# Taking a routing stage apart: choices inside the output stage, counts inside the first expert chunks, a residual add on GpSimd

## What is computed

```python
x = x + layernorm(attention(layernorm(x)))      # 16 heads, prefix mask
t = layernorm(x).reshape(-1, 256)
scores = softmax(t @ gate_w.T)                  # 8 experts
idx = top_k(scores + gate_b, 2)[1]              # the two best
cw = sum(one_hot(idx) * scores[idx])            # a weight per token and expert
y_e = swiglu((t @ w1_e.T + b1_e) * (t @ w3_e.T + b3_e)) @ w2_e.T + b2_e
out = x + layernorm(sum_e(cw_e * y_e) + shared_expert(t))
```

## Time and profile before

| | |
|---|---|
| time before, median of 3 runs | 2312.86 us (2309.55 to 2316.68) |
| the profiled execution, its own time | 2297.38 us |
| its span, from first to last instruction | 2295.6 us |
| TensorE matmul, busy | 2074.2 us, 90% |
| ScalarE, busy | 1701.4 us, 74% |
| VectorE, busy | 1521.9 us, 66% |
| GpSimd, busy | 645.4 us, 28% |
| output stage, about | 1253 to 1406 us |
| routing stage, about | 1406 to 1443 us |
| expert stage, matmuls | 1443 to 2234 us |

### The profile page before, as it was taken

How to read it: one execution, slowest core, us unless ns; L and a number is a source line. 1 busy time by engine, 2 the same in 40 slices (tenths; PEclk the granted TensorE clock), 3 DMA queues, 4 the chain that set the end, 5 groups by cost and what they waited for, 6 DMA issues and landing times. The chain is left out here.

```text
span 2295.6 us, 38125 instructions
## 1 busy us (share of the span) xinstructions
PE 2074.2 (90%) x14085; PEld 1267.4 (55%) x14085; DVE 1521.9 (66%) x2352; ACT 1701.4 (74%) x2162; POOL 645.4 (28%) x639
## 2 busy tenths in 40 slices
PE   5995999999999999999998794799999999999970
PEld 4783333333333333333332784688888888888860
DVE  4664255555555555555555896677789988998875
ACT  4663999999999999999997672433466666666645
POOL 1111000000000000000000451677345565555637
PEclk9997999999999999999999996899999999999995
DMA  5886655555444456555410682455567676677756
GB/s 184 307 290 194 139 104 105 105 102 90 73 87 87 90 100 105 105 102 75 58 37 21 220 272 108 164 179 173 193 194 208 179 179 176 173 182 178 175 167 254
DMA packets 162651, 340.50 MB, mean 148 GB/s; under 512 B 17768, under 2 KB 91624, under 8 KB 155176
## 3 DMA queue, kind: packets, MB, share of 16 engines
q1 hardware_dynamic: 130220, 284.42, 46.5%
q0 software_dynamic: 29936, 45.90, 10.7%
q10 hardware_dynamic: 2316, 7.80, 1.0%
HBM read 194.29 MB, written 143.62 MB: 147 GB/s over the span
## 5 line engine op out<-in xcount | busy, mean ns | idle before, releaser
L1108 ACT ACTIVATE att_prob<-att_scores 128x1024 f32<-128x1024 f32 (+2 forms) x1122 | 997.7, 1031 | 58.5 <-PE att_scores L1054 54.9
L1073 PE MATMUL att_out<-att_prob,att_va 128*32 128x512 f32 (+3 forms) x5000 | 576.5, 541 | 12.9 <-DVE att_prob L1140 12.9
L1054 PE MATMUL att_scores<-att_qs,att_ks 50*128 50x512 f32 (+3 forms) x2560 | 465.5, 430 | 21.2 <-DMA att_qs<-guard 17.1
L1054 PEld LDWEIGHTS att_scores<-att_qs,att_ks 50*128 50x128 f32 x2560 | 210.9, 185 | 492.5 <-ACT att_prob L1108 417.9
L1776 POOL DMA_INDIRECT sums<-moe_y,moe_token x142 | 290.9, 2048 | 265.5 <-ACT moe_y L2034 225.2
L1918 PE MATMUL moe_ps<-moe_xt_hi,moe_w_hi 128*128 128x512 f32 (+1 forms) x880 | 339.8, 386 | 10.1 <-ACT moe_h L2007 7.1
L1918 PE MATMUL moe_ps<-moe_xt_hi,moe_w_lo 128*128 128x512 f32 (+1 forms) x880 | 333.4, 379 | 0.0
L1918 PE MATMUL moe_ps<-moe_xt_lo,moe_w_hi 128*128 128x512 f32 (+1 forms) x880 | 331.9, 377 | 0.0
L1002 POOL DMA_DIRECT2D ctx_scr<-att_cout x64 | 55.1, 860 | 983.0 <-DVE att_cout L1190 944.1
L1140 DVE SCALAR_TENSOR_TENSOR att_prob<-att_prob,att_tri 128x512 f32<-128x512 f32 x224 | 144.8, 688 | 269.0 <-ACT att_prob L1108 269.0
L1073 PEld LDWEIGHTS att_out<-att_prob,att_va 128*32 128x32 f32 x5000 | 108.3, 108 | 186.3 <-issue 105.5
(11 more groups left out here) (259 smaller groups left out, 3257.5 us busy)
## 6 DMA issues: line engine op xcount, KB each, us to landing
qk_parts<-proj_qk SPq DMA_DIRECT2D x64, 512.0 KB, 4.2
keep_first_weights<-w_experts SPq DMA_DIRECT2D x22, 1412.0 KB, 6.6
moe_wraw<-w_experts SPq DMA_DIRECT2D x21, 1412.0 KB, 6.8
att_qs<-qk_parts SPq DMA_DIRECT2D x180, 128.0 KB
att_ks<-qk_parts SPq DMA_DIRECT2D x180, 128.0 KB
rows_in<-att_zeros SPq DMA_DIRECT2D x13, 1632.0 KB, 21.6
moe_rows<-rows_in SPq DMA_DIRECT2D x22, 544.0 KB, 3.8
proj_xin<-x SPq DMA_DIRECT2D x16, 512.0 KB, 3.8
```

Source lines behind the costliest of these rows:

```text
L1054: last = nc.tensor.matmul(pss[e % SBUFS][:, h, at:at + CH - q0], ks[s][rows, half, kt * P:(kt + 1) * P], qs[s][rows, half, c * CH + q0:(c ...
L1073: last = nc.tensor.matmul(pso[k % 2][strip, q0:], va[team % 2][:, kt, strip], probs_of(u)[:, h, at:at + CH - q0], start=(kt == 0), stop=(i ...
L1108: nc.scalar.activation(probs_of(u)[:, half * 2:half * 2 + 2, start:], pss[e % SBUFS][:, :, start:], ACT.Exp, scale=HD ** -0.5)\
```

## The change

- The routing stage is gone. Its tiles become pieces of one tile `late` (class `Routing`), which later is the place of sums.
- In the output stage VectorE makes softmax and choices for groups of 16 tiles (four chunks, 128x128 elements): for groups 0, 1 and 2 in steps 9 to 12, 13 to 16 and 17 to 20, behind `context_lo`: two instructions in the first of the four steps, then four, six and seven. The last group gets only its first two there. The logits lie in two PSUM tiles by turns. ScalarE takes the exponential of each group.
- The residual add goes from VectorE to GpSimd, as the last thing of GpSimd's step: `residual(k - NORM)`, that is chunk k-2. VectorE begins its step with `measure_sum(k-3)`, which waits for that.
- The first weights are loaded in step 2, the first rows in step 6, and the first weights are cut into parts in steps 17 and 18 (`CUT_AT`).
- In the expert stage VectorE first finishes the choices of the last group (17 instructions) with the parts of the first rows between them. TensorE counts behind block 0 of chunk 0 and transposes the rows of chunk 1 only then. Everything behind the counts is put into VectorE's chunks 0 to 2 behind single blocks (`route(c, f)`). GpSimd's scatters wait for `slots_known`, which comes behind block 2 of chunk 1. The eight prefix scans are one scan.
- `follow_products` lets scatters begin from block 8 on, and asks the last of them for the same block as before.

```diff
@@ attention_out, block.gpsimd @@
+                def residual(c):
+                    n, s = divmod(c, 2)
+                    pool.wait_ge(a_normed, (c + 1) * TPC)
+                    pool.wait_ge(x_loaded[s], n * 16 + 16)
+                    if n:
+                        pool.wait_ge(x1_stored[s], n * 16)
+                        pool.wait_ge(x_normed, (c - 1) * TPC)
+                    nc.gpsimd.tensor_tensor(x1[s][:], an[s][:], xin[s][:], ALU.add).then_inc(x1_done, 1)
...
                 for k in range(STEPS):
                     if chunk(k - ADD):
                         roots(1, k - ADD)
                     if chunk(k - PROJECT):
                         roots(0, k - PROJECT)
+                    if chunk(k - NORM):
+                        residual(k - NORM)
@@ attention_out, block.scalar @@
+                    g = group_at(k, 0)
+                    if g is not None:
+                        act.wait_ge(shifted, g + 1)
+                        nc.scalar.activation(r.ex[:, group_tiles(g)], r.ex[:, group_tiles(g)], ACT.Exp).then_inc(exped, 1)
+                    if k == CUT_AT:
+                        act.wait_ge(w_loaded[0], 16)
+                        nc.scalar.activation(w_first[0][:, 0:W13], first_raw[:, 0:W13], ACT.Copy).then_inc(w_hi[0], 1)
@@ attention_out, block.vector @@
-                    V.tensor_tensor(x1[s][:], an[s][:], xin[s][:], ALU.add).then_inc(x1_done, 1)
+                def measure_sum(c):
                     dve.wait_ge(x1_done, c + 1)
-                    measure(1, c, x1[s])
+                    measure(1, c, x1[c % 2])
...
                 for k in range(STEPS):
                     if chunk(k - ADD):
-                        residual(k - ADD)
+                        measure_sum(k - ADD)
                     if chunk(k - PROJECT):
                         add_bias(k - PROJECT)
                     if chunk(k):
                         context_lo(k)
+                    g = group_at(k, 0)
+                    if g is not None:
+                        shift_logits(g)
...
+                    g = group_at(k, 2)
+                    if g is not None:
+                        best_of(V, r, group_tiles(g), 0, then)
...
+                    if k == CUT_AT:
+                        dve.wait_ge(w_hi[0], 1)
+                        V.tensor_tensor(w_first[1][:, 0:W13], first_raw[:, 0:W13], w_first[0][:, 0:W13].bitcast(F32),
+                                        ALU.subtract).then_inc(w_lo[0], 1)
@@ experts @@
+        BEHIND = 2
 
         def follow_products(pool, q):
 
-            blocks = (q - LEAD) * (FIRST - 1) * FB // SCATTERS
+            blocks = (q - LEAD) * (FIRST - 1 - BEHIND) * FB // SCATTERS + BEHIND * FB
...
+                pool.wait_ge(slots_known, 1)
                 for i in range(NCH):
@@ experts, block.tensor @@
                     if prv is None:
                         turn(0, 0)
+                        hidden(0, 0, range(0, 1))
+                        count()
+                        turn(*nxt)
+                        hidden(0, 0, range(1, FB))
+                        return
@@ experts, block.vector @@
+                def picked_rows():
+                    for rank in range(2):
+                        then(V.tensor_tensor(r.tmp[:, rank], r.hot[:, rank], r.at, ALU.mult))
+                    then(V.tensor_reduce(r.slotf, r.tmp, AX_X, ALU.add))
+                    V.tensor_copy(slot[:], r.slotf).then_inc(slots_known, 1)
...
+                def route(c, f):
+                    if (c, f) == (0, 1):
+                        ranks()
+                    if (c, f) == (0, 2):
+                        bases()
+                    if (c, f) == (0, 3):
+                        jumps()
+                    if (c, f) == (1, 0):
+                        rows_of_tokens()
+                    if (c, f) == (1, 2):
+                        picked_rows()
+                    if (c, f) == (2, 1):
+                        owners()
+                    if (c, f) == (2, 3):
+                        chosen()
```

More of the change, by code:

```diff
@@ L1223, in _, with __init__, take @@
                                 power_of(late_of(u), half, half, stage)
-def attention_out(nc, ident, power, minus_one, wo, gw, x_ch, ctx_ch, x1_scr, tok_ch, logits,
-                  first_cin, bias, first_loaded):
+GROUPS = BCH
+GT = NT // GROUPS
+LATE = 7 * 2 * TPC * D
+class Routing:
+    def __init__(self, late):
+        self.late, self.used = late, 0
+        take = self.take
+        self.gb, self.lane = take(E), take(E)
+        self.top, self.den, self.best, self.first = take(NT), take(NT), take(NT), take(NT)
+        self.ex, self.score, self.biased, self.equal, self.place, self.both = (take(NT, E) for _ in range(6))
+        self.hot = take(2, NT, E)
+        self.before, self.onesq = take(P), take(P)
+        self.at, self.over = take(NT, E), take(NT, E)
+        self.total, self.upto, self.keeps = (take(E, NT) for _ in range(3))
+        self.tmp = take(2, NT, E)
+        self.cnt, self.padded, self.ends, self.base, self.odd, self.odds, self.single, self.jump = (
+            take(E) for _ in range(8))
+        self.cnti, self.shr = take(E).bitcast(I32), take(E).bitcast(I32)
+        self.ones = take(E)
+        self.room = take(1)
+        self.slotf = take(2, NT)
+        self.chunk0 = take(ROUTED)
+        self.past = take(ROUTED, E + 1)
+        self.alone = take(ROUTED, E)
+        self.mine = take(ROUTED, E)
+        self.eidf = take(NEC)
+    def take(self, *shape):
+        n = 1
+        for d in shape:
+            n *= d
+        piece = self.late[:, self.used:self.used + n]
+        self.used += n
+        assert self.used <= LATE
+        if len(shape) == 2:
+            return piece.rearrange("p (a b) -> p a b", b=shape[1])
+        if len(shape) == 3:
+            return piece.rearrange("p (a b c) -> p a b c", b=shape[1], c=shape[2])
+        return piece
@@ L1264, in attention_out, with group_at @@
         STEPS = NCH + LOGITS
+        CUT_AT = NCH + 1
+        def group_at(k, later):
+            g, at = divmod(k - LOGITS - later, BCH)
+            return g - 1 if at == 0 and 1 <= g < GROUPS else None
         def chunk(c):
@@ L1653, in experts @@
         acc[PAIRS - 1] = [chunks_in(half[:].rearrange("p k t -> p (k t)"), 1)[:, 0] for half in (sig, a)]
-        early_x1 = [ph.sb(f"x1_{i}", [P, 2, TPC, D])[:] for i in range(EARLY)]
+        early_x1 = places[3:]
         x1 = [[x[:, i] for i in range(2)] for x in early_x1] + [
@@ L1936, in down, with count @@
                         last.then_inc(y_done[s], 1)
+                def count():
+                    pe.wait_ge(marked, 1)
+                    both = r.both.rearrange("p t e -> p (t e)")
+                    for left, psum in ((r.before, psY[0]), (r.onesq, psY[1])):
+                        nc.tensor.matmul(psum[:].rearrange("p v d -> p (v d)"), left, both,
+                                         start=True, stop=True).then_inc(counted, 1)
                 def step(n, s, nxt, prv):
```

352 lines of the change are left out of this document (173 added, 179 removed).

## The result

The changed kernel takes 2352.4 us, median of four runs (2348.6 to 2356.2); the kernel before took 2313.6 beside it. The ratio is 1.017 with a 95% interval of 1.015 to 1.0189: 38.8 us slower. The forecast was 2358, 45.1 us slower.

The account below looks back on a forecast made before the run. It took GpSimd's add loop to bound the output stage and late scatters to bound chunk 14; 3.4 + 39.2 + 2.5 = 45.1 us on 2312.9 gave 2358 us, with 8 in 10 between 2326 and 2376.

Parts of the forecast that it names:

- The loop: Output stage: VectorE's next step waits for GpSimd's add, a round trip of 9.55 us a step for 7.58, 25.6 us more.
- Chunk 13's sum: Output stage: VectorE's step for this sum begins 32.5 us later, at 1409.3, from 25.6 + 3.5 + 3.4.
- The stage's end: End of output stage: the expert stage begins at 1446.6 instead of 1443.2, 3.4 us later.
- The new wait behind the cut: Output stage's end: `measure_sum(15)` queues on VectorE behind the first weights' conversion, a new wait of 4.1 us.
- Slots: Expert stage: `slots_known` comes 43.3 us after its begin; before, the first scatter went out at 1.0 us.
- The scatters: Expert stage: 128 scatters take 185.0 us at GpSimd's own pace, so chunk 14's turn comes at 234.6 us, 39.2 later.
- The restart: Expert stage, chunk 14: after standing 26 us TensorE restarts at 1.2 GHz, costing 2.5 us.
- The 15.5 us: Whole kernel: the median of the runs lies 15.5 us above the profiled execution of 2297.4 us.
- GpSimd's share in the shared chunks: Shared chunks: GpSimd busy 141.5 of 188.4 us, claimed as the highest share it has anywhere.
- Rival 4: Output stage: TensorE falls to 1.2 GHz in longer pauses, +31 us more at worst, 2389; chance 5%.
- the signs in the profile: Adds 9.5 us apart, VectorE idle before measuring, expert stage's first matmul near 1447, first scatter about 43 us behind, one TensorE pause.
- The one pause of 20 to 30 us ahead of `turn(14)`: Expert stage: TensorE stands once before transposing chunk 14's gathered rows, released by their load; none would mean wrong by 26 us.

Follow-up runs that it names:

- `aligned`: Changed kernel with 8 more floats of padding, so the first weights begin at multiples of 64 bytes in SBUF; 2337.5 us, ratio 1.0171.
- the reordered residual: GpSimd's residual add placed between its two groups of roots, not after both; on the changed kernel 2308.5 us, ratio 1.0045.
- `late_cut`: Changed kernel with residual between root groups, routing at once in chunk 0, scatters not held back, weights 64-byte aligned, weights cut at output stage's end; 2307.5 us, ratio 0.9977.
- late scatters: Kernel before with only GpSimd's scatters held back until TensorE has done three column blocks of chunk 2; 2335.2 us, ratio 1.0164.
- the reordered residual alone: Kernel before with only the residual moved to GpSimd, between its two groups of roots; 2307.5 against 2312.4 us, ratio 0.9972.

## Why the prediction was right

By its own steps, in order. Measured numbers of the expert stage are of `aligned`, where no gap stands in the way; those of the output stage are of the changed kernel, and `aligned` has the same to 0.1 us.

- **The loop.** 9.55 us a step forecast, 9.44 measured. Its add was taken from another stage at 2.34 and is 2.40 here. The Trainium skill's page "GPSIMD Engine Reference" (section "Engine selection"), which spoke against this edit, is borne out in its figure: 2.40 to 1.215 us is 1.98 times, its half speed. But the lower speed is the smaller part of the cost: with the same add elsewhere in the order the kernel is 29 us faster.
- **Chunk 13's sum** is measured at 1409.46; forecast 1409.3. That this is so close is partly luck. The forecast has chunk 0's sum ready at 1278.2 + 3.5 = 1281.7, and it is measured at 1283.58, 1.9 us later; thirteen steps of 9.44 are 1.4 us shorter than its thirteen of 9.55. They make 122.7 of the 125.9 us between the two sums. The other 3.2 stand mostly in steps with choices, where 3.4 were forecast for what GpSimd's add and VectorE's two-input operations cost one another.
- **The stage's end.** Expert stage from 1447.2, forecast 1446.6. The new wait behind the cut is there: chunk 15's sum is ready at 1422.89 + 2.35 = 1425.24 and measured at 1429.36, 4.1 us later as forecast. With the reordered residual it is there as well, but the cut made earlier cost as much in another step (`late_cut`).
- **Slots.** 43.0 us into the stage, forecast 43.3; the scan of 512, an estimate of 1.3, took 1.22. TensorE stood 3.6 us for chunk 4's tokens, forecast 3.5.
- **The scatters.** 185.0 us were taken over from before; they took 180.6, 4.4 less. This is the term that was mis-sized. The 128 have the same form and the same 0.30 us between most of them, but some last longer than the usual 0.96: 20 over 1.3 us in the kernel before, 16 in `aligned`, 15 with late scatters. Longer scatters are 2.7 of the 4.4 us, pauses between them the other 1.8; what makes a scatter long was not found. Chunk 14's turn lies 229.7 us into the stage and not 234.6, and TensorE stands 20.2 us and not 26.
- **The restart.** 2.5 us: from chunk 14's turn to chunk 15's it is 17.16 us in place of 14.62. After that nothing is made up and nothing is lost, 642.2 against 642.3 us.

The rows for the sum, first transposes of the stage and chunk 15's turn, from the kernel before and then from `aligned`:

```profile
1443.40 1.94 PE L359 MATMUL moe_psT<-keep_ident,keep_first_rows 128*128 128x128 f32 x8 [19.94 <-PEq L116]
...
1653.26 1.03 PE L359 MATMUL moe_psT<-keep_ident,moe_rows 128*128 128x128 f32 x8
```

```profile
1447.23 1.94 PE L359 MATMUL moe_psT<-keep_ident,keep_first_rows 128*128 128x128 f32 x8 [2.92 <-PEq L116]
...
1694.11 1.03 PE L359 MATMUL moe_psT<-keep_ident,moe_rows 128*128 128x128 f32 x8
```

Sum: 3.8 for the begin (1447.2 against 1443.4), 34.5 for chunk 14 (229.7 against 195.2), 2.5 for the restart, -0.1 for the rest: 40.7 us, which is the difference of the spans, 2336.3 and 2295.6. The forecast had 3.4, 39.2 and 2.5. All of this is shown where the gaps are absent. The changed kernel's own two measurements fell where they are present. There the price, 38.8 us, is near the sum, but the wait at chunk 14 that the sum rests on does not show, because TensorE comes 7.3 and 2.0 us after the rows.

The 15.5 us that the forecast added from the profiled execution to the median of the runs are, by their size, the difference between the two sorts of chip; it did not know that. One reading in it is wrong and has no weight: GpSimd's share in the shared chunks is not its highest, since in the last stage, from 2240 to 2290 us, it is busy 41.8 of 50.

Rival 4, a falling clock, happened and cost nothing that the steps show: the granted clock went from 0.95 to 0.85 in the output stage, but TensorE was busy only 96.4 of 125.9 us, and the steps without choices stayed at the loop's 9.44. Of the signs in the profile, the adds' distance, VectorE's wait, the stage's begin and the first scatter came as written. The one pause of 20 to 30 us ahead of `turn(14)` is missing in both profiles of the changed kernel; only kernels on the other sort of chip show it.

## What to carry to other kernels

Where an operation moves to an idle engine, draw the round trip through that engine's program order before counting its time: on the kernel before, the same 2.4 us add cost 30 us last in the step and won 5 in the middle. Where a serial stage is dissolved into the next one, ask when its result is wanted, not whether TensorE is busy meanwhile: here 37 us of routing came first for the sake of 185 us of scatters with 3.5 us of slack behind them, and in the kernels where TensorE stood for the gathered rows it turned to them 185 to 189 us after the first scatter, wherever that lay. And put the profile of a changed kernel beside one of the old kernel from the same chip, or compare only the medians of runs made beside each other.

## What the runs showed of the hardware

- Four chips in two groups, 15 us apart for one kernel (2297.5 and 2297.9 against 2312.4 and 2313.3). In all six profiles with the longer times, and in none of the others, ScalarE waits up to 19.6 us and VectorE up to 14.2 for "remote"; in the changed kernel and in the reordered residual alone TensorE also starts products 1.4 us apart with nothing to wait for. All of it lies ahead of chunk 14 and beside scatters. But none of it lies in the first 45 us of the stage, although in the reordered residual alone the scatters run from its begin (from 1439.70 us; its first such wait ends at 1490). What makes the gaps was not found.
- TensorE's 512-column products follow one another at 0.233 us in the changed kernel and at 0.227 after its weights were moved by 32 bytes, by the program's layout from 32 bytes past a multiple of 64 onto one. Other operands moved with them.
- A VectorE operation with two inputs in SBUF that takes 0.29 us took 2.21 beside GpSimd's add; a 128x1024 add in float32 took 1.215 us on VectorE and 2.35 to 2.55 on GpSimd.
- The 128 scatters took 179.3 to 185.1 us wherever the gaps were absent, and 191.1 to 197.4 with them.
